# Centring an RWKV-style state ahead of the recurrence: a bonus added inside PSUM, two Vector passes less, and all queue orders written anew

## The chip, the cores and the metric

The kernel runs on one NeuronCore of a Trainium2 chip. The metric is the device time in microseconds (us) of one execution. The engines are named as in the profile: PE is TensorE, with its weight loads apart as PEld; DVE is VectorE, ACT is ScalarE, POOL is GpSimd, SP issues DMAs.

## The reference, cut to what matters

One layer of an RWKV-6 block: 64 sequences of 64 steps, width E = 256, in H = 32 heads of S = 8. Five mixed inputs (`x5`) are made from the normalised input and its shift; from them come k, w (decay), v, r and the gate g. Each head then carries a state of 8x8:

```python
def step(s, rkvw):
    a = k_t[:, :, :, None] * v_t[:, :, None, :]
    out = jnp.einsum('bhk,bhkd->bhd', r_t, u * a + s)
    return (a + w_t[:, :, :, None] * s, out)
...
a4 = att.reshape(b, l, H, S)
m = jnp.mean(a4, axis=-1, keepdims=True)
var = jnp.mean((a4 - m) ** 2, axis=-1, keepdims=True)
att = ((a4 - m) * jax.lax.rsqrt(var + EPS)).reshape(b, l, E) * gn_w + gn_b
x = x + att * g @ Wo.T
```

A second part follows (layernorm, shift, sigmoid gate, squared ReLU, `ffn_Wv`). The output `out` is linear in v and in the first state, both along d, the index over which the mean m is taken.

## The kernel before, in words

The 64 sequences are cut into nine chunks of 4, 6, 8, 8, 8, 8, 8, 8 and 6 sequences (256, 384 and 512 tokens). A chunk goes through three stages. The letters here name the chunks of one turn of the loop: **A** is the chunk in its first stage (layernorm, shift, mixes, projections), **B** the next older (its state is being scanned), **C** the one before (the end of its scan, group norm, Wo, second layernorm), **D** the oldest (the second part of the block).

Every engine runs a list written out by hand (`DVE_ORDER`, `PE_ORDER`, `ACT_ORDER`, `POOL_ORDER`, `SP_ORDER`) of pairs (stage, lag): in turn i it does each stage for chunk i - lag, in the order of the list, and it waits at semaphores inside the stage. So a stage that isn't ready holds up all that stands behind it on its engine.

- The scan of a chunk is done in four quarters q. On DVE: `a{q}` (L428, products of k and v into `kv[:, q % 2]`), `sc{q}` (L438, four scans along time), `rs{q}` (L446, times r). On PE: `S{q}` (L861) sums over k into the PSUM tensor `patt`. `kv` has two buffers, so `a{q}` waits for `S{q-2}`. On POOL `s0{q}` (L321) puts the first state into `kv`.
- The v of a chunk (P0 on PE, L730; `a_v` on ACT, L610) is stored to HBM (`vst`) and read back, repeated over the partitions, as `vrep` in two halves (`vl0`, `vl1`) of 2 MB each; `a0` waits for the first, `a1` for the second.
- The bonus: `CB` on PE (L850) sums u r k, `bonus` on DVE (L415) multiplies v by it.
- The end of the attention of a chunk: `att` on DVE (L455) adds `bonus` to `patt` and writes it to SBUF; `M` on PE (L871) takes the mean over each head with a 128x128 matrix; `cen` on DVE (L460) subtracts it; `sq` on ACT (L661) squares; `VR` on PE (L878) takes the mean of squares; `rstd` on ACT (L668, L670: Ln and Exp, a table load before each); `gate` on DVE (L467, L473) scales, shifts and multiplies by silu(g); `WO` on PE (L737); `res` on DVE (L481).
- The second part: `st2`, `nrm2` on ACT with `rd2` on POOL between (L532 to L563, L311), `T2` on PE (L722), `xn2` on ACT (L678), `shift2` on DVE (L487 to L492), `RR`, `KK`, `Y2` on PE, `out` on DVE (L501).

The semaphores that matter here are these: `S0` of a chunk waits for `att` of the chunk before, because `patt` has one copy; `att` waits for `WO` of the chunk before.

```python
def c_att(c, p):
    dve.wait_ge(summed, NQ * (c + 1))
    if c >= 1:
        dve.wait_ge(wo_done, c)
    dve.wait_ge(bonus_ready, c + 1)
```

Of the kernel before, what the change touches and what calls it, by code (L numbers as in the profile page):

```python
# [11 lines left out]
S = E // H  # L12
# [4 lines left out]
P = 128  # L17
# [29 lines left out]
SP_ORDER = [("lx", 2), ("vst", 3), ("sx2", 5), ("vl0", 3), ("vl1", 3), ("lr", 4)]  # L47
LAGS = 5
# [19 lines left out]
def build(nc, x, prev, s0, vecs, w1, w2, dw1, dw2, large, consts, out):  # L68

    vscr = nc.dram_tensor("v_scratch", [2, E * T], F32, kind="Internal").ap()  # L70
    with ExitStack() as ctx:
# [3 lines left out]
        def sem(name):  # L75
# [76 lines left out]
        kv_ready, state_ready, rs_ready = [sem(n) for n in ("kv_ready", "state_ready", "rs_ready")]  # L152
        att_ready, cen_ready, scaled, y_ready, x2_ready = [sem(n) for n in ("att_ready", "cen_ready", "scaled", "y_ready", "x2_ready")]
        mean2_ready, var2_ready, xhat2_ready, sx2_ready, xk_ready, xr_ready = [sem(n) for n in ("mean2_ready", "var2_ready", "xhat2_ready", "sx2_ready", "xk_ready", "xr_ready")]
        gated, out_ready, u_put, fv_put, ln_put = [sem(n) for n in ("gated", "out_ready", "u_put", "fv_put", "ln_put")]
        x2_stored, y_added, squared1, squared2 = [sem(n) for n in ("x2_stored", "y_added", "squared1", "squared2")]
        xn_ready, th_ready, v_ready, k_ready, thd_ready, r_ready = [sem(n) for n in ("xn_ready", "th_ready", "v_ready", "k_ready", "thd_ready", "r_ready")]
# [3 lines left out]
            sem(n) for n in ("t1_done", "w1_done", "x_done", "pv_done", "pk_done", "d1_done", "pr_done", "d2_done", "pg_done", "cb_done")]  # L161
        summed, mean_done, var_done, wo_done, t2_done, rr_done, kk_done, y2_done = [
            sem(n) for n in ("summed", "mean_done", "var_done", "wo_done", "t2_done", "rr_done", "kk_done", "y2_done")]

# [124 lines left out]
        def _(pool):  # L289
# [23 lines left out]
            def put_s0(c, q):  # L313
                j, half = divmod(q, HF)
                if c > 0 or q >= 2:

                    pool.wait_ge(summed, NQ * c + q - 1)
                if c == 0 and q == 0:
                    pool.wait_ge(in_s0, 16)
# [22 lines left out]
        @block.vector  # L342
        def _(dve):
            def a_shift(c, p):
# [102 lines left out]

            def c_att(c, p):
                dve.wait_ge(summed, NQ * (c + 1))
                if c >= 1:  # L450

                    dve.wait_ge(wo_done, c)
                dve.wait_ge(bonus_ready, c + 1)
                n = extent(c)[1]
                dve.tensor_tensor(att[:, :, 0:n], patt[:, :, 0:n], bonus[:, p, :, 0:n], ALU.add).then_inc(att_ready, 1)  # L455

            def c_center(c, p):
                dve.wait_ge(mean_done, c + 1)
                n = extent(c)[1]
                dve.tensor_tensor(att[:, :, 0:n], att[:, :, 0:n], pc[:, 0:1, 0:n].broadcast_to([P, JH, n]), ALU.subtract).then_inc(cen_ready, 1)  # L460

            def c_gate(c, p):

                dve.wait_ge(rstd_ready, c + 1)
# [31 lines left out]
            def c_out(c, p):  # L496
# [20 lines left out]
                **{f"rs{q}": (lambda c, p, q=q: b_read(c, p, q)) for q in range(NQ)},  # L517
                "att": c_att, "cen": c_center, "gate": c_gate, "res": c_res, "shift2": c_shift, "out": c_out}
            for i in range(NCH + LAGS):
# [5 lines left out]
        def _(act):  # L525
# [192 lines left out]
        def _(pe):  # L718
# [82 lines left out]
            def p_unit(c, p, n, name, freed, done):  # L801
                wait_x5(pe, c, n)
                if c == 0 and n in (0, 3):
                    pe.wait_ge(in_vk if n == 0 else in_rg, 16)
                if freed is not None:

                    pe.wait_ge(freed, c + 1)
# [34 lines left out]
            def cb(c, p):  # L842
# [8 lines left out]
                ins.then_inc(cb_done, 1)  # L851

            def sums(c, p, q):

                j, half = divmod(q, HF)
                pe.wait_ge(rs_ready, NQ * c + q + 1)
                if q == 0 and c >= 1:
                    pe.wait_ge(att_ready, c)
                nb, n = extent(c)[0:2]
                for d in range(G4):  # L860
                    ins = pe.matmul(patt[d * H:(d + 1) * H, j, 0:n], sum_k[:, half, :],  # L861
                                    kv[:, q % 2, d, 0:nb].rearrange("p b t -> p (b t)"), start=(half == 0), stop=(half == HF - 1))
                ins.then_inc(summed, 1)

            def mean(c, p):
                pe.wait_ge(att_ready, c + 1)
                if c >= 1:
                    pe.wait_ge(gated, c)
                n = extent(c)[1]
                for j in range(JH):  # L870
                    ins = pe.matmul(pc[:, 0, 0:n], head_mean, att[:, j, 0:n], start=(j == 0), stop=(j == JH - 1))  # L871
                ins.then_inc(mean_done, 1)

            def var(c, p):
                pe.wait_ge(sq_ready, c + 1)
                n = extent(c)[1]
                for j in range(JH):
# [22 lines left out]
            def y2(c, p):  # L900
# [14 lines left out]
                **{f"S{q}": (lambda c, p, q=q: sums(c, p, q)) for q in range(NQ)},  # L915
                "M": mean, "VR": var, "WO": wo, "T2": t2, "RR": rr, "KK": kk, "Y2": y2}
            for i in range(NCH + LAGS):
# [58 lines left out]
```

## Time and profile before

| what | value |
|---|---|
| median of 3 runs | 589.7 us (588.98 to 591.48) |
| the profiled execution's own time | 592.12 us |
| its span, first to last instruction | 590.3 us |
| busy: PE, DVE, ACT, POOL | 78%, 83%, 49%, 13% |
| mean granted TensorE clock | 0.921 of full speed |

A row of a group of instructions reads: line, engine, operation, output and inputs, shape, count, then busy time, mean ns of one, then the idle time of the engine just before them and what ended it. A row of the timeline reads: start in us from the start of the span, how long it took, engine, line, and what it was, with the idle time before it in brackets. Consecutive DVE instructions overlap a little in the records (one of 1.22 us starts the next 1.14 us later), so the distance of two starts is what one costs its engine.

### The profile page before, as it was taken

The page shows a single profiled execution, that of the slowest core. Times are in us where ns is not written, and L with a number is a line of the kernel's source. Part 1 is how long each engine was busy: PE and PEld are TensorE (multiplying, and loading weights), DVE is VectorE, ACT ScalarE, POOL GpSimd, SP SyncE. Part 2 cuts the span into 40 slices and gives each one's busy share as a digit, 9 for nine tenths or more (in the row PEclk, how much of TensorE's full clock was granted, in tenths as well). Part 3 has the DMA queues.
Part 4 walks back from the last instruction along what each step waited for, and adds up shares of the span by engine and source line. Part 5 has one row for each costly group of instructions (what it writes and reads, how often), then busy time and mean ns, then how long its engine had stood idle before and what let it go on. Part 6 is the DMA issues. An engine that isn't in the chain of part 4 may idle for free.

```text
span 590.3 us, 5701 instructions
## 1 busy us (share of the span) xinstructions
PE 459.1 (78%) x1952; PEld 254.6 (43%) x1952; DVE 489.1 (83%) x502; ACT 289.2 (49%) x623; POOL 75.7 (13%) x91
## 2 busy tenths in 40 slices
PE   0767787978798879977998889878988797456434
PEld 0553543634364436532653355334634473243222
DVE  1349889879999999999899999997999899866221
ACT  4253563467435752784365646554545543422341
POOL 0100101210122022201310111210120102100000
PEclk9997987998899899998898999988989799959859
DMA  8070661794399129942895179614990693100200
GB/s 296 37 180 14 145 149 37 152 217 121 63 222 234 34 47 217 218 90 38 198 221 113 36 169 226 131 36 96 207 197 1 143 221 64 36 28 0 36 0 27
DMA packets 26693, 69.33 MB, mean 117 GB/s; under 512 B 1576, under 2 KB 19624, under 8 KB 24232
## 3 DMA queue, kind: packets, MB, share of 16 engines
q1 hardware_dynamic: 19416, 54.55, 37.8%
q0 software_dynamic: 7248, 14.42, 13.9%
q8 instruction: 15, 0.25, 0.2%
q14 instruction: 14, 0.11, 0.1%
HBM read 46.15 MB, written 12.19 MB: 99 GB/s over the span
## 4 chain that ended last, share of the span: by engine, by line
PE 42%; DVE 26%; issue 17%; DMA 7%; ACT 6%; POOL 1%; SPq 0%; DVEq 0%; POOLq 0%
PE pa L730 12%; PE pc L737 9%; DVE kv L438 8%; DVE x L365 4%; DMA vrep<-v_scratch 3%; DVE kv L428 3%; DVE kv L446 3%; PE pc L730 3%; PE pc L878 3%; PE patt L861 3%; DMA v_scratch<-v_sb 3%; PE pa L768 2%; PE pb L756 2%; PE pc L722 2%; PE pb L768 2%
## 5 line engine op out<-in xcount | busy, mean ns | idle before, releaser
L438 DVE TENSOR_TENSOR_SCAN kv<-w_sb,kv 128x512 f32<-128x512 f32 (+2 forms) x144 | 146.3, 1086 | 0.0
L730 PE MATMUL pa<-x,large_sb 128*128 128x512 f32 (+2 forms) x288 | 129.8, 598 | 1.6 <-ACT xn L583 1.4
L730 PEld LDWEIGHTS pa<-x,large_sb 128*128 128x128 f32 x288 | 59.8, 214 | 65.0 <-issue 58.5
L428 DVE TENSOR_TENSOR kv<-vrep,k_sb 128x2016 f32<-128x2016 f32 (+2 forms) x36 | 72.6, 2016 | 6.0 <-DMA vrep<-v_scratch 5.3
L446 DVE TENSOR_TENSOR kv<-kv,r_sb 128x2048 f32<-128x2048 f32 (+2 forms) x36 | 72.8, 2045 | 0.0
L321 POOL COPY kv<-s_sb 128x32 f32<-128x32 f32 (+2 forms) x36 | 24.3, 678 | 327.5 <-PE patt L861 327.5
L768 PE MATMUL pb<-th,w_sb 32*128 32x512 f32 (+2 forms) x108 | 39.0, 660 | 24.2 <-DVE x L365 24.2
L365 DVE SCALAR_TENSOR_TENSOR x<-pb,vec_sb,sx 128x512 f32<-128x512 f32 (+2 forms) x72 | 46.1, 683 | 9.1 <-PE pb L768 4.9
L861 PE MATMUL patt<-kv,const_sb 128*32 128x512 f32 (+2 forms) x288 | 36.0, 590 | 13.7 <-DVE kv L446 13.7
L878 PE MATMUL pc<-sq,const_sb 128*128 128x512 f32 (+2 forms) x36 | 22.3, 756 | 23.4 <-ACT sq L661 23.4
L737 PE MATMUL pc<-large_sb,xr 128*128 128x256 f32 x128 | 33.5, 420 | 7.9 <-DVE xr L492 7.9
L737 PE MATMUL pc<-large_sb,att 128*128 128x256 f32 x128 | 31.5, 400 | 8.7 <-DVE att L473 8.7
L311 POOL TENSOR_TENSOR rs<-var,neg_half 128x4 f32<-128x4 f32 (+2 forms) x18 | 26.3, 1463 | 51.5 <-ACT var L539 51.5
L737 PEld LDWEIGHTS pc<-large_sb,att 128*128 128x128 f32 x128 | 24.7, 199 | 18.4 <-DVE att L473 11.6
L532 ACT ACTIVATE ob<-xres 128x256 f32<-128x256 f32 x32 | 12.9, 404 | 40.2 <-DVE xres L481 40.2
L737 PE MATMUL pc<-large_sb,sq 128*128 128x256 f32 x128 | 29.3, 381 | 4.0 <-ACT sq L699 4.0
L737 PEld LDWEIGHTS pc<-large_sb,xr 128*128 128x128 f32 x128 | 26.6, 214 | 12.7 <-DVE xr L492 8.7
L730 PE MATMUL pc<-xk,large_sb 128*128 128x512 f32 (+2 forms) x72 | 29.8, 558 | 2.2 <-ACT trr L690 2.2
L302 POOL DMA_DIRECT2D x<-xn x21 | 19.7, 937 | 77.1 <-DVE x L365 77.1
L737 PEld LDWEIGHTS pc<-large_sb,sq 128*128 128x128 f32 x128 | 24.2, 190 | 11.3 <-ACT sq L699 5.4
L768 PEld LDWEIGHTS pb<-th,w_sb 32*128 32x128 f32 x108 | 12.5, 202 | 37.8 <-DVE x L365 35.4
L690 ACT ACTIVATE trr<-pc 128x1024 f32<-128x1024 f32 (+2 forms) x9 | 8.3, 928 | 40.6 <-PE pc L737 40.6
(87 smaller groups left out, 730.9 us busy)
## 6 DMA issues: line engine op xcount, KB each, us to landing
vrep<-v_scratch SPq DMA_DIRECT2D x12, 2048.0 KB, 18.3
x<-xn POOLq DMA_DIRECT2D x18, 512.0 KB, 7.7
vrep<-v_scratch SPq DMA_DIRECT2D x4, 1536.0 KB, 10.8
x_tok<-in_x SPq DMA_DIRECT2D x6, 512.0 KB, 24.6
v_scratch<-v_sb SPq DMA_DIRECT2D x12, 256.0 KB
xres<-in_x SPq DMA_DIRECT2D x6, 512.0 KB, 22.4
out<-xres SPq DMA_DIRECT2D x6, 512.0 KB, 10.3
out<-trr POOLq DMA_DIRECT2D x6, 512.0 KB, 9.5
```

What stands on the lines that cost most here:

```text
L302: pool.dma_start(x5[:, x5_slot(n), :, 0:nt], xn[:, c % 2, :, 0:nt], accum_op=ALU.add).then_inc(x5_added[n], 16)
L311: pool.tensor_tensor(rs[:, 0:n], var[:, 0:n], neg_half[:, 0:n], ALU.pow).then_inc(done, 1)
L321: pool.tensor_copy(kv[:, q % 2, :, 0:nb, 0], s0_sb[:, half, G4 * j:G4 * (j + 1), FIRST[c]:FIRST[c] + nb]).then_inc(s0_put, 1)
L365: return dve.scalar_tensor_tensor(out=x5[:, x5_slot(n), a, 0:nt], in0=src[:, 0:nt], scalar=vec(f"maa{g}", a), in1=sx[:, a, 0:nt], op0=ALU. ...
L428: dve.tensor_tensor(kv[:, q % 2, :, 0:nb, 1:L], vv[:, G4 * j:G4 * (j + 1), :, 0:L - 1], kk, ALU.mult).then_inc(kv_ready, 1)
L438: ins = dve.tensor_tensor_scan(flat, w_sb[:, p, q % HF, 0:nb].rearrange("p b t -> p (b t)"), flat, 0.0, ALU.mult, ALU.add)
L446: dve.tensor_tensor(flat, flat, r_sb[:, p, q % HF:q % HF + 1, 0:n].broadcast_to([P, G4, n]), ALU.mult).then_inc(rs_ready, 1)
L730: ins = pe.matmul(dst[:, m, 0:n], w(a)[:, m * P:(m + 1) * P], src[:, a, 0:n], start=(a == 0), stop=(a == HF - 1))
L737: ins = pe.matmul(pc_tok[:, t], src[:, a, t * P:(t + 1) * P], w(a), start=(a == 0), stop=(a == HF - 1))
L768: return pe.matmul(dst[:, 0:nt], w2_sb[rows, a * P:(a + 1) * P], th[rows, 0, 0:nt], start=True, stop=True)
L861: ins = pe.matmul(patt[d * H:(d + 1) * H, j, 0:n], sum_k[:, half, :], kv[:, q % 2, d, 0:nb].rearrange("p b t -> p (b t)"), start=(half == ...
L878: ins = pe.matmul(pc[:, 1, 0:n], head_mean, sq[:, j, 0:n], start=(j == 0), stop=(j == JH - 1))
```

## The change

`Wv` (in SBUF, once) and the first state (once) have the mean over each head subtracted on DVE. v, the state and so every sum over it are then centred, and `M` and `cen` go. The bonus (a product with the centred v) is no longer added on DVE: `BO` on PE multiplies it by the identity into `patt` with `start=True`, and the sums `S{q}` accumulate on it with `start=False`; `att` goes. `sq` and the first half of `gate` read `patt` (PSUM) directly, so `BO` of a chunk must wait for `scaled` of the chunk before, that is for the first half of its `gate`. All five orders are new. The core of the diff:

```diff
-DVE_ORDER = [("a3", 3), ("mix4", 2), ("sc2", 3), ("sc3", 3), ("rs2", 3), ("rs3", 3), ("rk", 2), ("out", 4),
-             ("att", 3), ("a0", 2), ("bonus", 2), ("cen", 3), ("shift", 1), ("sc0", 2), ("a1", 2), ("gate", 3),
-             ("rs0", 2), ("mix0", 1), ("res", 3), ("mix1", 1), ("sc1", 2), ("mix2", 1), ("rs1", 2), ("a2", 2),
-             ("mix3", 1), ("shift2", 3)]
-PE_ORDER = [("P4", 2), ("W1", 1), ("X01", 1), ("WO", 3), ("S0", 2), ("X2", 1), ("P0", 1), ("X3", 1), ("S1", 2),
-            ("T2", 3), ("P1", 1), ("X4", 1), ("RR", 3), ("D1", 1), ("KK", 3), ("D2", 1), ("P3", 1), ("Y2", 3),
-            ("S2", 2), ("S3", 2), ("CB", 1), ("T1", 0), ("M", 2), ("VR", 2)]
-ACT_ORDER = [("w", 2), ("r", 2), ("nrm", 1), ("xn", 1), ("sq", 3), ("rstd", 3), ("tg", 2), ("th", 1),
-             ("st", 0), ("st2", 3), ("v", 1), ("nrm2", 3), ("xn2", 3), ("k", 1), ("rr", 3), ("thd", 1),
+DVE_ORDER = [("rs1", 3), ("shift2", 4), ("mix4", 2), ("sc2", 3), ("a3", 3), ("rs2", 3), ("sc3", 3), ("rs3", 3),
+             ("rk", 2), ("out", 4), ("a0", 2), ("shift", 1), ("bonus", 2), ("sc0", 2), ("gate", 3), ("rs0", 2),
+             ("mix0", 1), ("mix1", 1), ("res", 3), ("a1", 2), ("a2", 2), ("mix2", 1), ("sc1", 2), ("mix3", 1)]
+PE_ORDER = [("X01", 1), ("BO", 2), ("WO", 3), ("S0", 2), ("P0", 1), ("X2", 1), ("X3", 1), ("T2", 3), ("P1", 1),
+            ("X4", 1), ("S1", 2), ("RR", 3), ("D1", 1), ("KK", 3), ("D2", 1), ("P3", 1), ("S2", 2), ("Y2", 3),
+            ("T1", 0), ("S3", 2), ("CB", 1), ("VR", 2), ("P4", 1), ("W1", 0)]
+ACT_ORDER = [("w", 2), ("r", 2), ("xn", 1), ("sq", 3), ("rstd", 3), ("tg", 2), ("th", 1), ("st", 0),
+             ("st2", 3), ("v", 1), ("nrm2", 3), ("xn2", 3), ("k", 1), ("rr", 3), ("thd", 1), ("nrm", 0),
              ("kk", 3)]
-POOL_ORDER = [("rd2", 4), ("s03", 3), ("ad3", 2), ("ad4", 2), ("rd1", 1), ("ad0", 1), ("s00", 2), ("ay", 4),
-              ("s01", 2), ("s02", 2), ("ad1", 1)]
-SP_ORDER = [("lx", 2), ("vst", 3), ("sx2", 5), ("vl0", 3), ("vl1", 3), ("lr", 4)]
+POOL_ORDER = [("s02", 3), ("s03", 3), ("ad4", 2), ("s00", 2), ("ad0", 1), ("s01", 2), ("ad1", 1), ("rd1", 0),
+              ("ay", 4), ("rd2", 3), ("ad3", 1)]
+SP_ORDER = [("vl1", 4), ("vst", 3), ("lx", 1), ("vl0", 3), ("sx2", 5), ("lr", 4)]
...
+            def center_wv():
+                dve.wait_ge(in_vk, 16)
+                for a in range(HF):
+                    wv = weight("Wv", a).rearrange("p (d h) -> p d h", h=H)
+                    total = rstd[:, a * H:(a + 1) * H]
+                    dve.tensor_reduce(out=total, in_=wv.rearrange("p d h -> p h d"), axis=mybir.AxisListType.X,
+                                      op=ALU.add).then_inc(wv_summed, 1)
+                    dve.wait_ge(wv_summed, a + 1)
+                    dve.scalar_tensor_tensor(out=wv, in0=total.unsqueeze(1).broadcast_to([P, S, H]), scalar=-1.0 / S,
+                                             in1=wv, op0=ALU.mult, op1=ALU.add).then_inc(wv_centered, 1)
...
@@ a_shift, after its last instruction
+                if c == 0:
+                    center_wv()
@@ a_bonus
-                    dve.wait_ge(att_ready, c - 1)
+                    dve.wait_ge(bonus_put, c - 1)
@@ b_products
+                if c == 0 and q == 0:
+                    center_s0()
...
-            def c_att(c, p):
-            def c_center(c, p):
...
             def c_gate(c, p):
                 dve.wait_ge(rstd_ready, c + 1)
+                if c >= 1:
+                    dve.wait_ge(wo_done, c)
                 n = extent(c)[1]
                 for j in range(JH):
-                    ins = dve.scalar_tensor_tensor(out=att[:, j, 0:n], in0=att[:, j, 0:n], scalar=vec("gn_w", j),
+                    ins = dve.scalar_tensor_tensor(out=att[:, j, 0:n], in0=patt[:, j, 0:n], scalar=vec("gn_w", j),
...
             def c_sq(c, p):
-                act.wait_ge(cen_ready, c + 1)
+                act.wait_ge(summed, NQ * (c + 1))
+                if c >= 1:
+                    act.wait_ge(y2_done, c)
                 n = extent(c)[1]
-                act.activation(sq[:, :, 0:n], att[:, :, 0:n], ACT.Square).then_inc(sq_ready, 1)
+                act.activation(sq[:, :, 0:n], patt[:, :, 0:n], ACT.Square).then_inc(sq_ready, 1)
...
+            def bonus_in(c, p):
+                pe.wait_ge(bonus_ready, c + 1)
+                if c >= 1:
+                    pe.wait_ge(scaled, c)
+                n = extent(c)[1]
+                for j in range(JH):
+                    ins = pe.matmul(patt[:, j, 0:n], ident, bonus[:, p, j, 0:n], start=True, stop=False)
+                ins.then_inc(bonus_put, 1)
...
@@ sums
-                if q == 0 and c >= 1:
-                    pe.wait_ge(att_ready, c)
@@ mean goes; var gets its wait for gated
```

`center_s0` does the same as `center_wv` on `s0_sb` (two halves of 512 elements a partition) and waits for the load of the state; the first `s00` on POOL waits for it, and the first `P0` on PE waits for `wv_centered`.

## Rows read from the trace of the kernel before

**Rows 1.** The page: busy time; DVE in 40 slices; the chain that ended last.

```profile
PE 459.1 (78%) x1952; PEld 254.6 (43%) x1952; DVE 489.1 (83%) x502; ACT 289.2 (49%) x623; POOL 75.7 (13%) x91
...
DVE  1349889879999999999899999997999899866221
...
PE 42%; DVE 26%; issue 17%; DMA 7%; ACT 6%; POOL 1%; SPq 0%; DVEq 0%; POOLq 0%
```

**Rows 2.** Busy time by stretch (us): length, engines, then PEclk, DMA share, GB/s.

```profile
39.60:538.90 499.30, 414.55 (x1748) 223.97 (x1748) 468.12 (x467) 258.63 (x546) 70.71 (x77) 0.92 0.56 124
312.50:372.60 60.10, 53.09 (x225) 28.28 (x224) 59.48 (x56) 34.51 (x75) 10.42 (x10) 0.97 0.61 136
372.60:435.50 62.90, 54.79 (x224) 28.61 (x223) 59.46 (x56) 33.23 (x70) 9.56 (x11) 0.95 0.59 127
```

**Rows 3.** Waits of DVE from 39.6 to 538.9: total us, times, longest.

```profile
DVE sq L487 <- ACT xn L678: 16.7, 8, 5.8
DVE kv L428 <- DMA vrep<-v_scratch: 5.3, 2, 2.8
```

**Rows 4.** Groups of instructions by line, all chunks together.

```profile
L455 DVE TENSOR_TENSOR att<-patt,bonus 128x1024 f32<-128x1024 f32 (+2 forms) x9 | 9.9, 1105 | 1.3 <-PE patt L861 1.2
L460 DVE TENSOR_TENSOR att<-att,pc 128x1024 f32<-128x1024 f32 (+2 forms) x9 | 9.9, 1100 | 2.8 <-PE pc L871 2.8
L871 PE MATMUL pc<-att,const_sb 128*128 128x512 f32 (+2 forms) x36 | 15.4, 551 | 1.7 <-DVE att L455 1.7
```

**Rows 5.** The same, each shape apart: a PSUM and an SBUF input.

```profile
L365 DVE SCALAR_TENSOR_TENSOR x<-pb,vec_sb,sx 128x512 f32<-128x512 f32 x48 | 33.6, 742 | 0.9 <-PE pb L768 0.9
L467 DVE SCALAR_TENSOR_TENSOR att<-att,vec_sb,rstd 128x512 f32<-128x512 f32 x12 | 8.5, 748 | 0.8 <-ACT rstd L670 0.8
```

**Rows 6.** Timeline of PE, two turns: P0 fast and slow, VR fast and slow.

```profile
335.51 3.70 PE L730 MATMUL pa<-x,large_sb 128*128 128x512 f32 x8
...
376.08 1.98 PE L878 MATMUL pc<-sq,const_sb 128*128 128x512 f32 x4 [2.40 <-ACT sq L661]
...
394.30 1.83 PE L768 MATMUL pb<-th,w_sb 32*128 32x512 f32 x4 [2.52 <-DVE x L365]
396.05 6.35 PE L730 MATMUL pa<-x,large_sb 128*128 128x512 f32 x8
...
438.98 3.66 PE L878 MATMUL pc<-sq,const_sb 128*128 128x512 f32 x4 [2.59 <-ACT sq L661]
```

**Rows 7.** Timeline of ACT around the second layernorm of the second turn.

```profile
402.44 1.02 ACT L610 ACTIVATE v_sb<-pa 128x1024 f32<-128x1024 f32 x1 [5.34 <-PE pa L730]
```

**Rows 8.** Timeline of DVE in that turn: res, and the wait of shift2.

```profile
391.71 1.22 DVE L481 TENSOR_TENSOR xres<-xres,pc 128x1024 f32<-128x1024 f32 x1
...
408.97 0.19 DVE L487 TENSOR_TENSOR sq<-prev_sb,xn 128x16 f32<-128x16 f32 x1 [3.26 <-ACT xn L678]
```

**Rows 9.** SP's DMA issues of the third chunk's v: store, then both loads.

```profile
103.76 1.17 SPq L226 DMA_DIRECT2D v_scratch<-v_sb  x2
...
115.17 1.35 SPq L239 DMA_DIRECT2D vrep<-v_scratch  x2
```

**Rows 10.** The page: a DMA's size and median us from issue to landing.

```profile
vrep<-v_scratch SPq DMA_DIRECT2D x12, 2048.0 KB, 18.3
```

**Rows 11.** Timeline of DVE at the start: where the centrings will stand.

```profile
19.89 0.88 DVE L365 SCALAR_TENSOR_TENSOR x<-pa,vec_sb,sx 128x256 f32<-128x256 f32 x2 [5.52 <-PE pb L768]
...
39.64 1.21 DVE L428 TENSOR_TENSOR kv<-vrep,k_sb 128x1008 f32<-128x1008 f32 x1 [2.84 <-DMA vrep<-v_scratch]
...
43.49 2.43 DVE L438 TENSOR_TENSOR_SCAN kv<-w_sb,kv 128x256 f32<-128x256 f32 x4
```

**Rows 12.** Timeline of DVE at the end: the last chunk's att, cen and gate.

```profile
544.43 0.96 DVE L455 TENSOR_TENSOR att<-patt,bonus 128x768 f32<-128x768 f32 x1 [0.24 <-PE patt L861]
547.04 0.95 DVE L460 TENSOR_TENSOR att<-att,pc 128x768 f32<-128x768 f32 x1 [1.65 <-PE pc L871]
552.96 1.15 DVE L467 SCALAR_TENSOR_TENSOR att<-att,vec_sb,rstd 128x384 f32<-128x384 f32 x2 [4.97 <-ACT rstd L670]
```

More of the change, by code:

```diff
@@ L152, in build @@
         kv_ready, state_ready, rs_ready = [sem(n) for n in ("kv_ready", "state_ready", "rs_ready")]
-        att_ready, cen_ready, scaled, y_ready, x2_ready = [sem(n) for n in ("att_ready", "cen_ready", "scaled", "y_ready", "x2_ready")]
+        bonus_put, scaled, y_ready, x2_ready = [sem(n) for n in ("bonus_put", "scaled", "y_ready", "x2_ready")]
         mean2_ready, var2_ready, xhat2_ready, sx2_ready, xk_ready, xr_ready = [sem(n) for n in ("mean2_ready", "var2_ready", "xhat2_ready", "sx2_ready", "xk_ready", "xr_ready")]
         gated, out_ready, u_put, fv_put, ln_put = [sem(n) for n in ("gated", "out_ready", "u_put", "fv_put", "ln_put")]
+        wv_summed, wv_centered, s0_summed, s0_centered = [sem(n) for n in ("wv_summed", "wv_centered", "s0_summed", "s0_centered")]
         x2_stored, y_added, squared1, squared2 = [sem(n) for n in ("x2_stored", "y_added", "squared1", "squared2")]
@@ L161, in build @@
             sem(n) for n in ("t1_done", "w1_done", "x_done", "pv_done", "pk_done", "d1_done", "pr_done", "d2_done", "pg_done", "cb_done")]
-        summed, mean_done, var_done, wo_done, t2_done, rr_done, kk_done, y2_done = [
-            sem(n) for n in ("summed", "mean_done", "var_done", "wo_done", "t2_done", "rr_done", "kk_done", "y2_done")]
+        summed, var_done, wo_done, t2_done, rr_done, kk_done, y2_done = [
+            sem(n) for n in ("summed", "var_done", "wo_done", "t2_done", "rr_done", "kk_done", "y2_done")]
         rk, kk_buf, xhat2, sx2, e_buf = th, sq, ob, sq, mix
@@ L318, in put_s0 @@
                 if c == 0 and q == 0:
-                    pool.wait_ge(in_s0, 16)
+                    pool.wait_ge(s0_centered, HF)
                 nb = extent(c)[0]
@@ L343, in _, with center_s0 @@
         def _(dve):
+            def center_wv():
[8 more added lines that the diff above has]
+                                             in1=wv, op0=ALU.mult, op1=ALU.add).then_inc(wv_centered, 1)
+            def center_s0():
+                dve.wait_ge(in_s0, 16)
+                for a in range(HF):
+                    state = s0_sb[:, a]
+                    total = rstd[:, (a + 1) * B:(a + 2) * B]
+                    dve.tensor_reduce(out=total, in_=state.rearrange("p d b -> p b d"), axis=mybir.AxisListType.X,
+                                      op=ALU.add).then_inc(s0_summed, 1)
+                    dve.wait_ge(s0_summed, a + 1)
+                    dve.scalar_tensor_tensor(out=state, in0=total.unsqueeze(1).broadcast_to([P, S, B]), scalar=-1.0 / S,
+                                             in1=state, op0=ALU.mult, op1=ALU.add).then_inc(s0_centered, 1)
             def a_shift(c, p):
@@ L446, in b_read, with c_gate @@
                 dve.tensor_tensor(flat, flat, r_sb[:, p, q % HF:q % HF + 1, 0:n].broadcast_to([P, G4, n]), ALU.mult).then_inc(rs_ready, 1)
-            def c_att(c, p):
-                dve.wait_ge(summed, NQ * (c + 1))
+            def c_gate(c, p):
+                dve.wait_ge(rstd_ready, c + 1)
                 if c >= 1:
                     dve.wait_ge(wo_done, c)
-                dve.wait_ge(bonus_ready, c + 1)
-                n = extent(c)[1]
-                dve.tensor_tensor(att[:, :, 0:n], patt[:, :, 0:n], bonus[:, p, :, 0:n], ALU.add).then_inc(att_ready, 1)
-            def c_center(c, p):
[L458 to L464, printed above, removed]
                 n = extent(c)[1]
                 for j in range(JH):
-                    ins = dve.scalar_tensor_tensor(out=att[:, j, 0:n], in0=att[:, j, 0:n], scalar=vec("gn_w", j),
+                    ins = dve.scalar_tensor_tensor(out=att[:, j, 0:n], in0=patt[:, j, 0:n], scalar=vec("gn_w", j),
                                                    in1=rstd[:, 0:n], op0=ALU.mult, op1=ALU.mult)
@@ L517, in _ @@
                 **{f"rs{q}": (lambda c, p, q=q: b_read(c, p, q)) for q in range(NQ)},
-                "att": c_att, "cen": c_center, "gate": c_gate, "res": c_res, "shift2": c_shift, "out": c_out}
+                "gate": c_gate, "res": c_res, "shift2": c_shift, "out": c_out}
             for i in range(NCH + LAGS):
@@ L804, in p_unit @@
                     pe.wait_ge(in_vk if n == 0 else in_rg, 16)
+                if c == 0 and n == 0:
+                    pe.wait_ge(wv_centered, HF)
                 if freed is not None:
@@ L861, in sums, with var @@
                     ins = pe.matmul(patt[d * H:(d + 1) * H, j, 0:n], sum_k[:, half, :],
-                                    kv[:, q % 2, d, 0:nb].rearrange("p b t -> p (b t)"), start=(half == 0), stop=(half == HF - 1))
+                                    kv[:, q % 2, d, 0:nb].rearrange("p b t -> p (b t)"), start=False, stop=(half == HF - 1))
                 ins.then_inc(summed, 1)
-            def mean(c, p):
-                pe.wait_ge(att_ready, c + 1)
+            def var(c, p):
+                pe.wait_ge(sq_ready, c + 1)
                 if c >= 1:
                     pe.wait_ge(gated, c)
[L869 to L875, printed above, removed]
                 n = extent(c)[1]
@@ L915, in _ @@
                 **{f"S{q}": (lambda c, p, q=q: sums(c, p, q)) for q in range(NQ)},
-                "M": mean, "VR": var, "WO": wo, "T2": t2, "RR": rr, "KK": kk, "Y2": y2}
+                "BO": bonus_in, "VR": var, "WO": wo, "T2": t2, "RR": rr, "KK": kk, "Y2": y2}
             for i in range(NCH + LAGS):
```

## The prediction

> **What bounds the kernel now.** I read the page first. DVE is the busiest engine, 489.1 of 590.3 us, and in its 40 slices the reader sees 8s and 9s from the fourth to the thirty-fourth [rows 1]. The chain that ended last gives PE 42% and DVE 26% [rows 1]: that doesn't say that PE bounds, it says that the two hand work to each other all the time (a mix needs a projection, a projection the mix before).
>
> The table of stretches tells more. From the first products (39.6 us) to the last read of the last chunk (538.9 us) DVE is busy 468.1 of 499.3 us, PE 414.6 [rows 2]. So DVE has only 31.2 us of idle time in the whole body, and PE 85. Two full turns of the loop beside each other show it best: 60.1 us with DVE busy 59.48, and 62.9 us with DVE busy 59.46 [rows 2]. DVE's work is the same, the turn that is longer has 3.4 us of idle time, and its granted clock is 0.95 against 0.97. So the body is DVE's work (59.5 us a turn) plus what it waits.
>
> What does it wait for? Over half, 16.7 us, is `shift2` waiting for `xn2` on ACT [rows 3]. In the long turn: PE finds a gap of 2.52 us, the next P0 takes 6.35 us where the same eight matmuls took 3.70 a turn earlier [rows 6] (1.2 in place of 2.4 GHz for part of it), `v` on ACT waits 5.34 us for it [rows 7], `nrm2` and `xn2` stand behind `v` in ACT's list, and `shift2` starts 17.3 us after the start of `res` and has idled 3.26 [rows 8]. Any DVE work taken away counts nearly in full as long as PE, ACT and the v loop keep the pace; that is what has to be checked.
>
> **The change, part by part.**
>
> *att and cen go.* They are busy 9.9 us each over nine chunks [rows 4], 19.8 in all. The last chunk's two (0.96 + 0.95 [rows 12]) belong to the tail: 17.9 left in the body. Back to back each costs 0.09 less than it lasts (1.22 against a distance of 1.14), 16 of them 1.4. Body: **-16.5**, in a full chunk 2.28. Their own waits go too: 1.3 and 2.8 us before them, less the 1.9 of the last chunk [rows 4, 12]: **-2.2**.
>
> *M becomes BO.* `M` is 36 records, 15.4 us [rows 4]; `BO` is as many 128-deep matmuls of as many columns, 15.4 us. `start=False` in the sums adds no instruction. PE: 0.
>
> *gate and sq read PSUM.* The trace has both cases for this DVE form at 512 columns: with an input in PSUM 742 ns, all in SBUF 748 [rows 5]. I take 0. The Trainium skill, "VectorE: DVE Perf Modes", section "The TRN2 errata", has a fixed cost of 120 cycles with a PSUM source against 58, at 0.96 GHz; that would be 65 ns more for each of 18 instructions, 1.2 us, and the saving would be that much smaller. The rows here don't show it.
>
> *The centrings.* Neither reduction is in the trace. Of `Wv`: two reductions of 256 elements and two scalar_tensor_tensor. Below, a reduction costs what the 0.44 us instruction of 256 elements does (half of the 0.88 pair), above, a quarter of the 2.43 us of four 256-element scans, 0.61 [rows 11]: 1.8 to 2.1 us, in a wait of 5.52 us of DVE for the first mixes [rows 11]: 0; without that cover, 2. Of the state, 512 elements wide: two at 0.75 (as in rows 5) and two at 0.75 to 1.2 (twice the scan): 3.0 to 3.9, in front of `a0` of the first chunk, where DVE now waits 2.84 us for `vrep` [rows 11]. The POOL copies `s00`, `s01` of this chunk now wait for it, and the first scan for them; they are short and the scan starts 3.9 us after `a0` [rows 11]. Moreover, `nrm` of the second chunk now stands ahead of the first chunk's `w` and `r` on ACT (some 1 us later `rk`), and the x load `lx` (512 KB) goes between the store of v and `vl0` on SP; it could cost `vl0` between nothing and a quarter of the 18.3 us that 2 MB take [rows 10]. The three delays overlap. I take **+2** for the start; ends 0 and +4.
>
> *The new loop over patt.* Before, `patt` was free once `att` had copied it. Now `BO` waits for the first half of the previous `gate`, and behind `BO` on PE stand `WO`, `S0`, P0 and all the rest. I laid the new lists out over a turn with the measured durations, from `rs1` of C at 0. DVE without a wait takes 59.5 - 2.3 = 57.2 us: `sc2` at 7.5, `rs3` ends 23, `rk` 23, `out` 24, `a0` 25.4, `shift` 27.6, `gate` 35.8, `rs0` ends 40.8, `mix0` 40.8, `res` 44.7, `a2` 48, `mix2` 50.2, `mix3` 56. PE has `S3` of C at about 25.2. From `sq` to `gate` the chain took 4.97 us for 384 tokens [rows 12]; for 512 and behind `xn` and `CB` I get `rstd` at 31.7. `gate` has 4 us in hand, `S0` ends at 44 and `a2` wants it at 48. The cost is 0, and past 4 us of delay on PE it counts in full.
>
> *xn2.* `rs1` (2.2 us) now stands between `mix3` and `shift2`, and `v` comes after `st2`, so that a slow P0 no longer delays `nrm2`. From the start of `res` to `shift2` DVE has 14.8 us of own work; the chain took 17.3 with a slow P0 of which 3.2 were waited [rows 8], so about 14. Of the 16.7 us, 5.8 are the last chunk but one, in the thin end, and stay; of 10.9 I leave 3: **-7.9**.
>
> *New gaps on PE.* `X2` and `X3` now stand together, with P0 in front and not between them; `mix2` (1.3 us) falls between. Then `T2` waits for the layernorm. Between P0's end (47.6) and P1's start (55.8) PE has only 3 us of work. After gaps of 2.4 to 2.6 us the trace shows half clock in two cases of three (P0 6.35 us, VR 3.66 against 1.98; after the third gap VR took 1.98) [rows 6]. So I expect P1 to be slow in many turns, 2.7 us late. On the other hand the gap in front of `VR` closes. A late P1 makes `Y2` late, and `out` (DVE, at 24) waits up to 2 us. Below 0, above 2 us in each of seven turns: 14. Two rows in three speak for slow, hence I take three turns of 2: **+6**.
>
> The Trainium skill has a rule on this, "TensorE: Matmul & The Clock Gate", section "HAM oscillation": the gate lets half the pulses through after idleness and opens with sustained matmuls. By it the denser half of the turn (P1 to P4) keeps 2.4 GHz and the thin one loses it; the rows agree, as the slow groups stand behind gaps.
>
> *Tail.* Between the start of `att` (544.43) and the end of `cen` (548.0) lie 3.6 us, all in the last chunk's chain [rows 12]. `sq` now follows `S3` itself. The rest of the chain is unchanged: **-3.6**. (`S2` of the last chunk also moves ahead of `Y2`, under 1 us.)
>
> *The v loop.* From the v store's issue to that of the load it took 11.4 us [rows 9], then 18.3 to landing for 2 MB [rows 10]: 29.7 us. `v` is now ready some 3 us later in the turn (after `st2`), `a0` wants it 31.5 us after that. (51.2 and 57.2 + 25.4 in the layout). Hidden, with 2 us in hand.
>
> **Sum**: -16.5 - 2.2 - 7.9 - 3.6 + 2 + 6 = -22.2. Against the profiled execution, 592.1 - 22.2 = 569.9; the median of the runs is 2.4 us lower, so 589.7 - 22.2 = 567.5, and I say 567.5.
>
> **The rivals.**
>
> *DVE never waits* (0.17). No slow P1, no late `out`: the +6 goes, and the start costs nothing, and the 3 us left to `xn2` go too: -22.2 - 6 - 2 - 3 = -33.2, some 556.5. For: PE has 85 us idle in the body. Against: half clock after gaps.
>
> *The v loop decides* (0.12). `lx` ahead of `vl0` adds up to a quarter of 18.3, 4.6 us: 34.3 against 31.5, so `a0` waits 2.8 us in each of six full turns: +17, 584. For: DVE waited for `vrep` already in two places, 5.3 us [rows 3]. Against: `vl0` no longer shares with the x2 store ahead of it.
>
> *patt and PE together* (0.15). With a slow P1 and also slow `Y2` and `VR` (+2.65, as P0, and +1.7 [rows 6]), `rstd` is late past the 4 us in hand, and `gate` and `out` wait 2 us in all seven turns: +8 over my +6, and a little in `a2`: 578.
>
> *Slower* (0.04): TensorE's clock. PE's work in a turn is 51 us at full clock by the durations that I laid out, and 2.4 us it can't avoid waiting (`th`, `mix2`). Half clock through a quarter of the turn would add 13, and the turn is 66, more than today's 61.5 (the mean of the two in rows 2): seven times 4.5 more, 589.7 + 31 - 3.6 + 2, about 619. It decides from 8.6 us of loss a turn, a granted clock of about 0.86 in the body, where it is 0.92 [rows 2].
>
> *No difference that can be measured* (0.03): several of these at half size. What is removed is removed; only a new wait could eat it.
>
> The forecast itself has 0.49, with a range of its own of 562 to 573. No measurement of this kernel tells less than about 0.5% (3 us) from no change. Range of 8 in 10: 557 to 582, from DVE never waiting to most of the v loop's case. Faster 0.93, same 0.03, slower 0.04.
>
> **What would show it.** DVE busy 489 - 20 + 5 = about 474 us; no rows at L455, L460, L871; a turn of 58 to 59.5 us in place of 60.1 and 62.9; waits of `shift2` under 10 us in all; P1 near 6 us in many turns, right after the gap. Wrong: `a0` waiting for `vrep` in each turn, `gate` waiting for `rstd`, or a body clock under 0.88.

## The result, and the profile after

The changed kernel takes 563.03 us (median of 4 runs, 559.31 to 566.44), the kernel before 590.49 us (4 runs). The ratio is 0.9547, 95% interval 0.9504 to 0.959: 4.5% faster, 27 us. Forecast were 567.5 us and a range of 557 to 582. The profiled execution took 566.1 us with a span of 564.2, against 590.3: 26.1 us less.

The page of the changed kernel (busy time, DVE in 40 slices), to be held against [rows 1]:

```profile
PE 466.0 (83%) x1952; PEld 262.4 (47%) x1952; DVE 475.4 (84%) x492; ACT 287.9 (51%) x623; POOL 92.8 (16%) x91
...
DVE  0428999999999999989999999999999999777221
```

DVE is 13.7 us less busy and still the busiest. Its 9s now fill the middle. Busy time by stretch: the start up to the first products, the body up to the last read of the last chunk, the tail, and one full turn:

```profile
0.00:46.97 46.97, 28.59 (x121) 21.16 (x122) 14.44 (x28) 18.80 (x51) 2.41 (x10) 1.00 0.56 165
46.97:516.90 469.93, 415.00 (x1754) 225.82 (x1752) 451.38 (x452) 255.54 (x543) 88.16 (x79) 0.92 0.59 129
516.90:564.20 47.30, 22.44 (x78) 15.40 (x78) 9.62 (x14) 13.61 (x29) 2.20 (x2) 0.81 0.11 19
299.10:356.94 57.84, 54.01 (x224) 28.84 (x223) 57.27 (x55) 34.48 (x74) 12.68 (x11) 0.94 0.65 140
```

Against [rows 2] the body went from 499.3 to 469.9 us (-29.4): 16.7 us are DVE work (468.1 to 451.4), 12.7 are its idle time (31.2 to 18.5). The tail went from 51.4 to 47.3 (-4.1). The start grew from 39.6 to 47.0 (+7.3). The sum of the unrounded numbers is -26.1. A full turn is 57.84 us, where it was 60.1 and 62.9. DVE's waits in the body, the counterpart of [rows 3]:

```profile
DVE xres L496 <- PE pc L754: 4.4, 2, 3.7
DVE sq L502 <- ACT xn L695: 3.9, 1, 3.9
DVE trr L516 <- PE pc L754: 3.7, 4, 1.8
```

`shift2` (its first instruction writes `sq`) waited eight times before, 16.7 us; now once, in the thin end. `vrep` is no longer waited for. On PE, the turn answering to [rows 6]: X3 behind the gap, P1 after it, and VR:

```profile
328.10 2.08 PE L785 MATMUL pb<-th,w_sb 32*128 32x512 f32 x4 [2.26 <-DVE x L389]
...
332.63 4.59 PE L747 MATMUL pa<-x,large_sb 128*128 128x512 f32 x8
...
362.58 1.88 PE L898 MATMUL pc<-sq,const_sb 128*128 128x512 f32 x4
```

The gap that was forecast is there (2.26 us in front of X3), and P1 behind it is slow, but less than forecast: 4.59 us in the turn shown and 4.53 to 5.53 in the six full turns, where 3.70 is full pace and 6.35 was feared. `out` (the waits of `trr` above) waits 3.7 us in all. In front of VR there is no gap any more.

The start is where some of the gain was lost again. This shows on DVE (the counterpart of [rows 11]) and on PE. DVE's rows show the two centrings, and the wait of `rk` for r:

```profile
14.27 0.58 DVE L349 TENSOR_REDUCE rstd<-large_sb 128x32 f32<-128x256 f32 x1
...
19.88 0.88 DVE L389 SCALAR_TENSOR_TENSOR x<-pa,vec_sb,sx 128x256 f32<-128x256 f32 x2 [3.61 <-PE pb L785]
...
43.01 0.69 DVE L432 TENSOR_TENSOR th<-r_sb,k_sb 128x512 f32<-128x512 f32 x1 [5.68 <-ACT r_sb L645]
43.62 1.03 DVE L360 TENSOR_REDUCE rstd<-s_sb 128x64 f32<-128x512 f32 x1
...
46.97 1.20 DVE L454 TENSOR_TENSOR kv<-vrep,k_sb 128x1008 f32<-128x1008 f32 x1
```

PE's row shows the first chunk's P1, with the same eight matmuls in 3.78 us that take 1.97 at full pace:

```profile
28.60 3.78 PE L747 MATMUL pa<-x,large_sb 128*128 128x256 f32 x8
```

### The profile page after: what moved, and what is told of

It reads as the page before. It is cut to its first block, busy times and chain, and to the rows that moved or that the text cites. A ratio compares the mean times of both kernels' runs of the same rounds, so it can differ in the third digit from the quotient of the medians.

```text
span 564.2 us, 5698 instructions
## 1 busy us (share of the span) xinstructions
PE 466.0 (83%) x1952; PEld 262.4 (47%) x1952; DVE 475.4 (84%) x492; ACT 287.9 (51%) x623; POOL 92.8 (16%) x91
## 4 chain that ended last, share of the span: by engine, by line
PE 46%; issue 24%; DVE 16%; ACT 8%; POOL 4%; DMA 1%; POOLq 0%; SPq 0%; DVEq 0%; ACTq 0%
PE pa L747 12%; PE pc L754 10%; DVE kv L464 4%; PE pc L747 4%; PE patt L888 3%; PE pb L814 3%; DVE x L389 3%; DVE kv L454 2%; POOL out L330 2%; PE pc L739 2%; PE pb L857 2%; PE pb L773 1%; PE pb L785 1%; PE pa L842 1%; ACT ob L578 1%
## 5 line engine op out<-in xcount | busy, mean ns | idle before, releaser
L747 PE MATMUL pa<-x,large_sb 128*128 128x512 f32 (+2 forms) x288 | 132.5, 609 | 2.8 <-DVE x L398 2.3
L747 PEld LDWEIGHTS pa<-x,large_sb 128*128 128x128 f32 x288 | 61.1, 219 | 64.0 <-issue 50.6
L321 POOL COPY kv<-s_sb 128x32 f32<-128x32 f32 (+2 forms) x36 | 37.3, 1038 | 185.2 <-PE patt L888 160.3
L311 POOL TENSOR_TENSOR rs<-var,neg_half 128x4 f32<-128x4 f32 (+2 forms) x18 | 29.7, 1652 | 67.5 <-ACT var L554 67.5
L739 PE MATMUL pc<-const_sb,ob 128*128 128x128 f32 x64 | 15.4, 415 | 23.1 <-ACT ob L578 23.1
L754 PEld LDWEIGHTS pc<-large_sb,att 128*128 128x128 f32 x128 | 26.5, 208 | 13.5 <-DVE att L488 6.4
## 6 DMA issues: line engine op xcount, KB each, us to landing
vrep<-v_scratch SPq DMA_DIRECT2D x12, 2048.0 KB, 13.9
```

The lines of the kernel that those rows point to most:

```text
L311: pool.tensor_tensor(rs[:, 0:n], var[:, 0:n], neg_half[:, 0:n], ALU.pow).then_inc(done, 1)
L321: pool.tensor_copy(kv[:, q % 2, :, 0:nb, 0], s0_sb[:, half, G4 * j:G4 * (j + 1), FIRST[c]:FIRST[c] + nb]).then_inc(s0_put, 1)
L739: ins = pe.transpose(dst[:, a, t * P:(t + 1) * P], src[:, t, a * P:(a + 1) * P], ident)
L747: ins = pe.matmul(dst[:, m, 0:n], w(a)[:, m * P:(m + 1) * P], src[:, a, 0:n], start=(a == 0), stop=(a == HF - 1))
L754: ins = pe.matmul(pc_tok[:, t], src[:, a, t * P:(t + 1) * P], w(a), start=(a == 0), stop=(a == HF - 1))
```

## The experiments

There were twelve runs, eleven of them of an edited kernel. Each is compared with runs of the kernel before on the same chip; the ratio, with its interval, is the number to go by. The first four shared a chip.

**The changed kernel once more**, no edit.

> The changed kernel itself, once more, on the chip of the next three. Its four runs fell in two pairs, 566.1 and 566.4, 559.3 and 560.0 us. Theory: the pairs differ in the start, where PE's matmuls ran at half pace from 14.5 to 41 us in the profile (P0 of the first chunk 3.78 us, 1.97 at full pace); expected here either about 566 with the first products (DVE, L454) at 47 us, or about 560 with them at 41 to 42. Rival: the pairs differ in the body; then the first products stand at the same place in both and the body (first products to last read) is 6 us shorter.

561.57 us (556.49 to 565.82), ratio 0.948 (0.9436 to 0.9523). Its profile has the shorter start, with a span of 554.6 us. First PE at the first P1 (the row above), then DVE at the first products, then its body by stretch:

```profile
27.00 1.99 PE L747 MATMUL pa<-x,large_sb 128*128 128x256 f32 x8
```

```profile
40.09 1.20 DVE L454 TENSOR_TENSOR kv<-vrep,k_sb 128x1008 f32<-128x1008 f32 x1
```

```profile
40.09:507.30 467.21, 411.76 (x1754) 224.49 (x1752) 451.08 (x452) 255.26 (x543) 89.28 (x79) 0.92 0.59 131
```

Of 9.6 us between the two spans, 6.9 lie ahead of the first products and 2.7 in the body; the tail is the same 47.3. So most of the difference between these two executions is the start: PE reaches full pace at about 25 us here, at about 41 in the first profile. The other executions have no profile; in the profiles of the later variants of the changed kernel without extra matmuls it is about 25, 32 or 41. With the short start the loss against [rows 11] is 0.5 us, with the long one 7.3.

What decides between them isn't visible in PE's work. In both profiles PE runs at half pace from its first matmul on, and its waits from the first transposes to the first P1 are the same: 2.98, 0.62, 1.71 and 0.98 us. Only one of the two then reaches full pace at 25 us.

**The removal with the old orders.** All five lists of the kernel before, less `att`, `cen` and `M`, with `BO` between `WO` and `S0`:

```diff
+PE_ORDER = [("P4", 2), ("W1", 1), ("X01", 1), ("WO", 3), ("BO", 2), ("S0", 2), ("X2", 1), ("P0", 1), ("X3", 1), ("S1", 2),
...
```

> The removal alone: the changed kernel's arithmetic with all five orders of the kernel before (BO put between WO and S0). Theory: the body loses 16.7 us of DVE work and the tail 4, the first products stand near 42.5 (the state's centring), and the waits of shift2 for xn2 (16.7 us before) stay or grow: 590.5 - 16.7 - 4 + 3 = 573, waits of shift2 over 12 us. Rival 1: the orders bring nothing, the removal is all: 563. Rival 2: under the old order gate and BO are late for S0 (patt has one copy) and the saving is lost: 585 or more, with a2 waiting for the sums.

571.14 us, ratio 0.9661 (0.9619 to 0.9703). As the theory had it. `shift2` kept its waits:

```profile
DVE sq L495 <- ACT xn L688: 13.7, 8, 5.8
```

The removal alone is 20 us, the orders on top of it 10 (0.9661 to 0.948; the intervals don't overlap).

**The new orders without the removal.** The kernel before, `att` placed ahead of `a0`, `cen` ahead of `sc0`, `M` ahead of `VR`; nothing is centred ahead.

> The orders alone: the kernel before with the new orders (att ahead of a0, cen ahead of sc0, M ahead of VR), no centring. Theory: DVE's work stays at 489, the xn2 waits fall by 12 us, the start loses about 4 by PE's pace: 590.5 - 12 + 4 = 582. Rival 1: without the removal the new order gives nothing, 590. Rival 2: it gives all, 565.

617.96 us, ratio 1.0463 (1.0427 to 1.0499): slower than before, which neither I nor a rival expected. DVE's waits from its first products (38.4 us) to its last read, at the first half of `gate` and at a mix:

```profile
DVE att L459 <- ACT rstd L662: 22.7, 8, 3.9
DVE x L357 <- PE pb L760: 13.9, 8, 2.7
```

On PE the gap in front of VR is 5.89 us long, and VR after it is slow:

```profile
331.59 3.43 PE L870 MATMUL pc<-sq,const_sb 128*128 128x512 f32 x4 [5.89 <-ACT sq L653]
```

The new orders put the end of the attention between `S3` and a `gate` 10 us later (25.2 and 35.8 in the layout of the prediction), and `P4`, `W1` and the next turn behind VR on PE. With `att`, `M` and `cen` still in the chain, it doesn't fit. A part of this is due to where I put `cen`: in the same turn `M` has ended at 325.7 us, but `cen`, behind `bonus` in DVE's list, starts only at 329.23:

```profile
323.82 1.88 PE L863 MATMUL pc<-att,const_sb 128*128 128x512 f32 x4
```

```profile
329.23 1.22 DVE L452 TENSOR_TENSOR att<-att,pc 128x1024 f32<-128x1024 f32 x1
```

So some 3.5 of the 5.89 us in front of VR are due to that place. The run shows that the orders are no gain of their own with the three stages in these places; other places weren't tried, so it doesn't show that no order of the old arithmetic could gain.

**The state centred early.** `center_s0()` called right after `center_wv()`.

> The state's centring moved from in front of the first products (43.6 to 47.0 us in the profile of the changed kernel) to right behind that of Wv (from 16.3 us), where DVE waited 3.61 us for the first mixes. Theory: it costs 3.4 us on the path where it stands, and 0 to 0.5 there: 3 us faster than the changed kernel of this call. Rival: vrep or r is late anyway and the first products don't move: no difference.

556.12 us, ratio 0.9404 (0.9361 to 0.9447), 5.4 us under the changed kernel beside it, though its profile had the long start. The direction is the theory's. With the same long start the first products stand at 43.58 us, 3.4 earlier than in the changed kernel's profile; this is the centring. The other 2 us have no cause shown. The two intervals (0.9361 to 0.9447, and 0.9436 to 0.9523) touch, so the 5.4 us are themselves uncertain.

**Extra matmuls at the start.** Results that nobody reads, written into `patt` before its first use: six ahead of the first stage, three behind the first transposes and three behind the first X01.

```diff
+            def warm(times):
+                for _ in range(times):
+                    pe.matmul(patt[:, 0, 0:2 * P], ident, const_sb[:, 0:2 * P], start=True, stop=True)
...
+            warm(6)
...
+                if c == 0:
+                    warm(3)
```

> The changed kernel with 12 extra matmuls in the first 21 us on PE (identity times constants, into patt, which nobody reads before the first sums overwrite it): 6 before the first transposes, 3 behind them, 3 behind X01 of the first chunk, all in gaps. Theory: the start loses time only where PE's matmuls run at half pace, in some executions till 41 us and in others till 25 us; kept busy, PE is at full pace from the first projections in every execution: first products at 38 to 40 us, times near the fast ones of the changed kernel (556 to 560), and the spread of the runs under half. Rival: the pace is a matter of chance that PE's load doesn't change; then 561 with the same spread, plus the 1 to 2 us by which the extra matmuls delay the first ones.

556.23 us (5 runs, 553.02 to 557.24, a spread of 4 us where six of the changed kernel had 9), ratio 0.9422 (0.94 to 0.9444). In its profile P0 and P1 of the first chunk run at full pace and the first products start at 35.59 us:

```profile
18.27 1.99 PE L747 MATMUL pa<-x,large_sb 128*128 128x256 f32 x8 [0.21 <-DVE x L398]
...
22.51 1.99 PE L747 MATMUL pa<-x,large_sb 128*128 128x256 f32 x8
```

In this execution PE is at full pace from its first work for the chunk on, as in no profile without the extra matmuls. The median is 5.3 us under the repeat and the ratio lower than that of the changed kernel's two measurements (0.9547 and 0.948), but the intervals of this run and the repeat (0.9436 to 0.9523) still touch. So the pace at the start very probably depends on PE's load; the last run below shows that this is not the whole of it.

**Both together.**

> The extra matmuls at the start and the state's centring in the early wait of DVE, together. Theory: both are at the start and of different engines, so they add up only where the first products then wait for neither r nor the centring but for vrep: 553 to 556, first products at 37 to 39 us. Rival: vrep is the bound at once; no better than the early centring alone (556).

555.35 us, ratio 0.9417 (0.9402 to 0.9433): no better than either alone. Its profile (559.0 us, the slowest of its six) shows how they get in each other's way. The early centring waits 1.13 us for the load of the state, the first mixes come late, and PE sits idle for 3.19 us in front of the first P0. The granted clock by stretch (the third number from the end) falls there:

```profile
14.00:18.00 4.00, 3.38 (x33) 2.19 (x31) 2.81 (x5) 2.96 (x13) 0.00 (x0) 1.00 0.68 285
18.00:22.00 4.00, 0.81 (x3) 0.54 (x3) 3.93 (x8) 0.60 (x3) 1.20 (x3) 0.79 0.00 2
22.00:26.00 4.00, 4.00 (x12) 2.49 (x10) 0.79 (x2) 0.60 (x1) 0.00 (x0) 0.50 0.00 0
```

0.50 is 1.2 of 2.4 GHz. P0 and P1 take the 3.78 us that the changed kernel's profile shows. Here half clock until about 40 us follows a stretch in which PE was idle. That the long start of the changed kernel is the same half clock is likely, since the same matmuls take the same 3.78 us; that such an idle stretch brings it about there is not shown, for the changed kernel waits only 1.71 us in front of P0, in both of its profiles.

**P0 between X2 and X3 again.**

> The changed kernel with P0 between X2 and X3 on PE, as in the order before, so that mix2 is covered by P0. Prediction's theory: X2 and X3 together make the gap that puts P1 at half clock; apart they save the late out, 2 to 4 us. Rival: P0 (and v, vrep, k behind it) starts later, X2 waits for mix1 and the gap only moves ahead of P0: no difference, or 1 to 5 us slower by waits of mix2 or a0.

561.16 us, ratio 0.9528 (0.9492 to 0.9564). No difference from the changed kernel (0.9547 and 0.948): the rival was right. The gap beside X2 and X3 is real, but putting P0 between them saves nothing that can be measured.

**Six more squares in each chunk**, some 6.4 us between `S3` and `VR`; the same values are written again.

```diff
+EXTRA = 6
...
+                for k in range(EXTRA):
+                    act.activation(sq[:, :, 0:n], patt[:, :, 0:n], ACT.Square).then_inc(late, 1)
+                    act.wait_ge(late, EXTRA * c + k + 1)
                 act.activation(sq[:, :, 0:n], patt[:, :, 0:n], ACT.Square).then_inc(sq_ready, 1)
```

> The changed kernel with the square of patt taken seven times in place of once in each chunk (the same values written again), 6.4 us more between S3 and VR. Theory: gate has 4 us in hand and VR stands ahead of P4 and W1 on PE, so some 2.5 to 5 us of the 6.4 come out in each of eight chunks, with gate waiting for rstd: 585 to 600. Rival: the loop over patt has no slack, 6.4 us in each chunk: 612 or more; or it has slack enough: under 570.

611.72 us, ratio 1.0378 (1.0357 to 1.0398). The squares are taken in all nine chunks; ACT is busy 338.0 us in place of 287.9, so 50.1 us were put in, and the time is 50 us longer than the repeat's 561.57 (49 to 53 by the ratios). All of it came out. That is at the edge of the first rival (no slack) and far outside my 585 to 600. DVE's wait is at `gate`:

```profile
DVE att L484 <- ACT rstd L692: 28.6, 7, 7.6
```

PE has a gap of 5.88 us in front of VR, after which VR takes 3.78 us in place of 1.88: the gap is paid twice. The next VR starts 65.0 us later, where a turn took 57.84: 7.1 us more for squares of 6.3. It is the same picture as in the run with the new orders alone.

**Two more squares**, 2.1 us.

> The changed kernel with the square of patt taken three times in each chunk, 2.1 us more between S3 and VR. Six more gave 50 us, 6.2 in each of eight chunks. Theory of the prediction: gate has 4 us in hand, so 2.1 us are hidden but for what PE's gap in front of VR costs: under 6 us in all, 563 to 567. Rival: PE as a whole has no slack either, and each microsecond in front of VR comes out: 8 x 2.1, 578.

567.03 us, ratio 0.9581 (0.9533 to 0.9629), 5.5 us over the changed kernel's repeat (measured at another time; by its interval apart from that repeat, not from the first measurement, whose interval reaches 0.959). The run with `nrm` moved, measured beside it, has 560.86 us, 6.2 less. 16.5 us were put in (ACT 304.4 against 287.9), and about a third came out. So the loop over `patt` has a few us in hand in each turn, as forecast, and 6.4 are past the end of them. The changed kernel's own trace says the same: in its full turns `rstd` ends 3.1 to 4.6 us before `gate` starts; in the turn shown above it ends at 367.1, and the row of `gate` is

```profile
370.59 1.39 DVE L482 SCALAR_TENSOR_TENSOR att<-patt,vec_sb,rstd 128x512 f32<-128x512 f32 x2
```

**rs1 behind shift2.**

> The changed kernel with rs1 behind shift2 on DVE, not in front of it. Theory of the prediction: shift2 then waits for xn2 again, about 1.5 to 2.5 us in each of seven turns: 571 to 578. Rival: the waits vanished because v stands behind st2 on ACT and res came earlier, and rs1's place matters little: within 3 us of the changed kernel.

571.34 us, ratio 0.969 (0.9653 to 0.9728): 1.5 to 2.2% over the changed kernel (0.9547 and 0.948), as the theory had it in size. But `shift2` waits only 8.0 us in all, 4.1 more than in the changed kernel's profile. As much again is at `out`, which waits 8.3 us and not 3.7, and on PE `S1` now waits for `rs1`:

```profile
PE patt L886 <- DVE kv L470: 15.1, 8, 7.3
```

**nrm where it was on ACT.**

> The changed kernel with nrm behind w and r on ACT again, one turn later, as before. Theory: only the start gains (r of the first chunk 1 to 2 us earlier) and the turns lose nothing or a little, since T1 stands behind Y2 on PE: 559 to 562. Rival: T1 waits for xhat in each turn, xn and sq stand behind it on ACT, and PE gets a gap: 570 or more.

560.86 us, ratio 0.95 (0.947 to 0.9531): no difference. `nrm`'s place makes no difference that can be measured.

**The best version.** Extra matmuls, and `center_s0()` at the head of the first `rk`, where DVE waits for r.

> The extra matmuls at the start as before, and the state's centring right in front of the first rk, where DVE waits for r (3.3 us in the kernel before, 5.7 in the changed kernel's profile), not in front of the first mixes, where it waited 1.1 us for the load of the state, made PE wait 3.19 us for the first P0 and the granted clock fell to 0.50 until 38 us. Theory: no gap for the clock to fall in and 2 to 3 us of the centring hidden: 552 to 555, first products at 33 to 36 us. Rival: the start's clock is chance in spite of the extra matmuls, median near 556 with single runs at 559.

555.05 us (549.83 to 557.83), ratio 0.9393 (0.9346 to 0.944), the lowest ratio of all but not apart from the other variants of the start (0.9404 to 0.9422). DVE's rows: `rk` waits for r only 0.40 us, but then the products wait for `vrep`.

```profile
34.37 0.69 DVE L434 TENSOR_TENSOR th<-r_sb,k_sb 128x512 f32<-128x512 f32 x1 [0.40 <-ACT r_sb L645]
37.15 1.21 DVE L454 TENSOR_TENSOR kv<-vrep,k_sb 128x1008 f32<-128x1008 f32 x1 [2.08 <-DMA vrep<-v_scratch]
```

So in this profile the centring is hidden and the first products wait for the v loop. This version beats both kernels: 36 us under the kernel before and, by the ratios, 5 to 9 under the changed one.

The expectation of "no gap for the clock to fall in" failed. PE had the same extra matmuls as in the first run with them, and after the first transposes the same waits (1.69 and 0.62 us); yet here the granted clock is 0.50 from 18 to 22 us. The extra matmuls behind X01 take 2.93 us, where they took 1.56, and P0 takes 2.77 in place of 1.99:

```profile
17.50 2.93 PE L932 MATMUL patt<-const_sb 128*128 128x256 f32 x6
20.22 2.77 PE L747 MATMUL pa<-x,large_sb 128*128 128x256 f32 x8
```

Full pace is back at 22 us. So the extra matmuls don't keep the clock up in every execution, and the rival that chance plays a part in spite of them is not out. Of the three profiles with extra matmuls one has no half clock up to P1, this one a short stretch, and the one with the wait of 3.19 us a long one.

## Why the prediction was right

The forecast of 567.5 us was 4.5 us too high. The mechanism was right: DVE's work left the time one for one, and the waits of `shift2` went. That the sum came so near the median was partly luck. In body and tail -24.2 were forecast and -33.5 found, 9.3 us more gained; at the start +2 were forecast and +7.3 found, 5.3 more lost. The two misses cancel in part. Point by point, against the profiled execution (-22.2 forecast, -26.1 found):

- *att and cen go*: -16.5 forecast, 16.7 us less DVE work in the body. Right, and the removal was run alone with the old orders (20 us with the tail).
- *M becomes BO, gate and sq on PSUM*: no cost. The first instruction of `gate` reads PSUM in 735 ns, SBUF in 748 [rows 5]. The extra 65 ns that would follow from the table in the Trainium skill, "VectorE: DVE Perf Modes", section "The TRN2 errata", are not there.
- *Idle time in the body*: -2.2 - 7.9 + 6 = -4.1 forecast, -12.7 found. Here are two mis-sized terms and a missing one. `xn2`'s waits went down by 12.8 us, not 7.9, and none is left in the full turns; `rs1`'s place has a part in it, as the run with `rs1` behind `shift2` shows, and `v`'s place was not tested apart. *New gaps on PE*, +6, was too dear: P1 is 0.8 to 1.8 us late in the full turns where I took 2.7, and `out` waits 3.7 us, 3.3 more than before. With P0 between X2 and X3 nothing was gained. Missing is the wait for `vrep`, which is gone. Of its 5.3 us [rows 3] only one wait of 2.44 us, at 128 us, lies in the body; the other is the 2.84 in front of the first products [rows 11].
- *The centrings and the start*: +2 forecast, +7.3 in the profile and +0.5 in the repeat. The centrings cost what was bounded. For `Wv` it is 2.0 us, hidden: the first mixes start at 19.88 us, before at 19.89 (a reduction takes 0.58 us, within the bounds of 0.44 and 0.61). For the state it is 3.4 us, in front of the first products, where the wait of 2.84 for `vrep` stood; the reductions of 1.03 us lie within 0.75 to 1.2. What I did not have in the sum at all is TensorE's pace at the start. It makes 6.9 us between two executions of this kernel. Extra load on PE made the start shorter in the profiles that had no long wait; what decides from one execution to the next stays open.
- *Tail*: -3.6 forecast, -4.1 found.
- *The new loop over patt*: no cost, with "4 us in hand" (3.1 to 4.6 in the trace). Right for 2 us of delay; at 6.3 us the loss was 7.1 in a turn, not the 2.3 that "past 4 us it counts in full" gives. PE's gap of 5.88 us in front of VR and a VR that is 1.9 us slower stand in that turn; how much of the loss is which was not separated.
- *The v loop*: in the turn shown, the store is issued at 327.5 and the load at 337.8, 10.3 us (11.4 before [rows 9]); the load then takes 13.9 us where it took 18.3 [rows 10]. The new orders do this, not the removal: 13.8 us with the new orders alone, 18.6 with the old ones. That the halves are no longer issued as a pair is my reading of it. `a0` starts at 360.1 and waits for nothing: 8 us in hand, where I had 2. The page's row:

```profile
vrep<-v_scratch SPq DMA_DIRECT2D x12, 2048.0 KB, 13.9
```

The rival "DVE never waits" (556.5 us) did about as well as the forecast: it is 6.5 us off the first median and 5.1 off the repeat's, the forecast 4.5 and 5.9. In body and tail it had -33.2, and -33.5 were found, though by another road: `out` does wait and P1 is slow. What it missed is the start, which it put at nothing. The rivals on the other side are out: `a0` doesn't wait for `vrep` in the body, `gate` doesn't wait for `rstd`, and the body clock is 0.92, as before. One sign named in advance did not come: P1 near 6 us in many turns.

Open are what decides TensorE's pace at the start, the cause of 2 of the 5.4 us that the early centring seemed to gain, and other places for `att`, `cen` and `M` in the new orders.

## What to carry to other kernels

A linear step (a mean, a bias) that stands behind a recurrence can often be moved to its inputs, once, or into the accumulation; what leaves the busiest engine came out of the time one for one here. What leaves the chain besides makes room for a tighter order: the order here is worth 10 us with the shorter chain and costs 27 with the long one, in the one placement that was tried. So an order is to be made anew after the removal, and not judged before it. And a start in which one engine waits for the next is worth a look of its own: twelve useless matmuls gave about 5 us, at the edge of what these runs can tell apart.

## What the runs showed of the hardware that was not expected

The granted clock's column says 1.00 in the first 40 us of the changed kernel's profile, while a P0 there takes 3.78 us for 1.97 us of work. From 22 to 26 us the row reads:

```profile
22.00:26.00 4.00, 4.00 (x12) 2.56 (x11) 0.96 (x2) 0.60 (x1) 0.19 (x1) 1.00 0.00 0
```

In the run with both edits of the start the same matmuls, equally slow, stand beside a clock of 0.50. There the column had already changed once, from 1.00 between 18 and 22 us. So in these traces a 1.00 ahead of the first change in the column is no evidence of full clock; the duration of a known group is the better sign.
